# The experts' second layer as seven block products of half depth in place of four plain ones

## The chip, the cores and the metric

The kernel runs on one core of one Trainium2 chip. The metric is the device time of one launch in microseconds; lower is better. Engines are called PE (TensorE), DVE (VectorE), ACT (ScalarE), POOL (GpSimd) and SP (SyncE); the weight load of PE is PEld.

## What is computed

Two blocks follow each other on `x` of 32 sequences of 64 tokens of 1024 features. Cut to what matters here:

```python
x = x + ffn0(cond0(x))                       # mixing inside each sequence, then up/gate, silu, down
base_in = x @ W + lora(x)                    # "lin"
base  = einsum('bsi,oi->bso', base_in, W_org)
q     = einsum('bi,ki->bk', base_in.mean(axis=1), Wq)
coeffs = softmax(einsum('bk,ek->be', q, lora_keys) / sqrt(K))
h     = einsum('bsi,eir->bser', base_in, lora_down)        # 8 experts x rank 64 = 512 rows
delta = einsum('be,bser,ero->bso', coeffs, h, lora_up)     # the experts' second layer
x = x + base + delta
```

The second layer is one matrix product: 1024 outputs, depth 512 (expert and rank together), over the tokens, after `h` was scaled by the coefficients.

## The kernel before

The tokens are taken in two halves `h` of 1024, each in two tiles of 512. A half goes through a mixing step and six stages, `up0`, `up1`, `down`, `lin`, `exp` and `expup` (`STAGES`, line 55). `exp` is the joint stage: the base product and the experts' first layer together, on the same activations. `expup` is the experts' second layer.

**Block products.** A stage's product is cut in 2 x 2 blocks and done with seven block products instead of eight, from sums of weight blocks (T1 = w12 - w11, T2 = w22 - T1, T3 = w22 - w12, T4 = w21 - T2) and sums of activation blocks (S1 = a2 + a3, S2 = S1 - a0, S3 = a0 - a2, S4 = a1 - S2). Product 0 is w11 with a0, 1 is w21 with a1, 2 is T2 with S2, 3 is T1 with S1, 4 is w22 with S4, 5 is T3 with S3, 6 is T4 with a3. Products 0, 2, 3 and 4 (`IN_X`, line 44) add up in the same four PSUM banks without clearing them, 6 adds onto 5; after each one DVE adds what the banks hold into the output block `TO_BLOCK[i]`. So PE may go on to a bank only when DVE has read it (`wait_bank_free`, line 642; line 684 for this case). `expup` is the exception: it has four plain products of depth 512, no sums and no carried banks; `UP_TO_BLOCK` (line 48) names their output blocks. Below E0 to E3 are those four.

**Float32 by three passes.** Each operand is split in a rounded part and a rest. ACT makes the rounded part (`s_hi` line 813 from activations, `t_hi` line 832 from weights), DVE the rest (`s_lo`, `t_lo`, line 902), and PE multiplies hi by hi, hi by lo and lo by hi (lines 638 to 640). A product has four groups of output rows (six in `exp`), a group has four pieces of the depth, so twelve matmuls of 512 columns. `s_hi`/`s_lo` have two slots, `t_hi`/`t_lo` four slots of 128x1024.

**Order of the work.** PE, DVE and ACT each run one hand-written loop over all products (`for n in range(LAST + 1)`; DVE at line 1087). In the turn of product n DVE does, in this order: the second half's add of product n-1 (`dve_after`), the `s_lo` of n+1, the first weight rest of n+1, scalings of `dve_post`, the activation sums (`s_sum`, line 921), the weight sums (`t_sum`, line 945; in `exp` they come after the next step and the second weight rest), the add of the first half of n (line 1000, which waits for two groups of PE), further weight rests, and the add of the second half if `dve_own` gives it. Queues are in order: what waits holds back all behind it. `exp` scales the four expert blocks by the coefficients (line 1041), three of them in the turn of its last two products and one after its last.

**Loads and stores.** SP issues the weight loads in the order of its loop (line 544), each behind a wait that says its buffer is free (`load_w`, line 464; `load_x`, line 502, brings the next half's tokens). Around `expup` of the first half the order is: "lower" and "upper" (the two halves of `lora_up`, in buffers 3 and 1), four `x` pairs, "21" and "11" of the next `up0`; then "22", the last four `x` pairs, "12". POOL stores each finished output half block (line 613).

**Between the halves.** After `expup` of the first half PE does the mixing of the second (line 721): eight pairs of sequences, two banks each. Pairs 0 and 1 go to banks 0 to 3, pairs 2 and 3 to banks 4 to 7, and each waits for DVE's add of the last product that used its banks (line 731). In the same turn DVE makes the weight sums T1 and T2 of the next `up0` before its add of the last product's halves.

Of the kernel before, what the change touches and what calls it, by code (L numbers as in the profile page):

```python
# [47 lines left out]
UP_TO_BLOCK = (0, 2, 3, 1)  # L48
# [8 lines left out]
PRODUCTS = [(s, i) for s in range(NSTAGE) for i in range(4 if STAGES[s][1] == "expup" else 7)]  # L57
# [9 lines left out]
def groups_in(n):  # L67
    return 6 if kind_of(n) == "exp" else 4

# [15 lines left out]
S_ID, S_LAST = {}, []  # L85
T_ID, T_LAST = {}, []
for _n, (_s, _i) in enumerate(PRODUCTS):
    _up = kind_of(_n) == "expup"
    if _up and _i >= 2:
        S_ID[_n] = S_ID[_n - (1 if _i == 2 else 3)]  # L90
    else:
        S_ID[_n] = len(S_LAST)
        S_LAST.append(_n)
    S_LAST[S_ID[_n]] = _n
    for _j in range(groups_in(_n) // 2):
        if _up and _i % 2 == 1:
            T_ID[_n, _j] = T_ID[_n - 1, _j]
        else:
            T_ID[_n, _j] = len(T_LAST)
            T_LAST.append(None)  # L100
        T_LAST[T_ID[_n, _j]] = (_n, 2 * _j + 1)


def s_new(n):
    return S_LAST.index(S_LAST[S_ID[n]]) == S_ID[n] and not (kind_of(n) == "expup" and PRODUCTS[n][1] >= 2)


def t_halves(n, when):


    if kind_of(n) == "expup" and PRODUCTS[n][1] % 2 == 1:
        return []
    found = []
    for j in range(groups_in(n) // 2):
        before = T_LAST[T_ID[n, j] - 4] if T_ID[n, j] >= 4 else (-2, 0)
        if when == (0 if before[0] < n - 1 else before[1] // 2 + 1):
            found.append(j)
    return found
# [4 lines left out]
def t_sums_beside(n):  # L123
# [3 lines left out]
    if kind == "exp":  # L127
        found += {0: [(s, "T2", 0), (s, "T2", 1), (s, "T1", 2)], 1: [(s, "T2", 2)],
                  2: [(s, "T3", 0), (s, "T3", 1), (s, "T3", 2)],
                  4: [(s, "T4", 0), (s, "T4", 1), (s, "T4", 2)]}.get(i, [])  # L130
    elif kind != "expup":
        found += {3: [(s, "T3", 0), (s, "T3", 1)], 4: [(s, "T4", 0), (s, "T4", 1)]}.get(i, [])
    to = None
# [6 lines left out]
    elif to is not None and STAGES[to][1] != "expup":  # L140
# [42 lines left out]
def dve_after(n):  # L183
# [4 lines left out]
    return [] if kind == "expup" and i == 3 else dve_half(n, 1)  # L188
# [10 lines left out]
def dve_own(n):  # L199

    kind, i = kind_of(n), PRODUCTS[n][1]
    if kind == "exp" or kind == "expup" and i == 3:
# [49 lines left out]
SUMMED_STAGES = [s for s in range(NSTAGE) if STAGES[s][1] != "expup"]  # L252


def s_at(s, name):
    return 4 * SUMMED_STAGES.index(s) + S_ORDER[name]


def build(nc, x_pairs, x_t, idx, cond_t, b_upgate, b_down, lora_a, lora_b, keys_t, wq_t,
# [3 lines left out]
    with ExitStack() as ctx:  # L263
# [38 lines left out]
        a_raw = r[:, 8, :].rearrange("p (t n) -> p t n", t=TILES)  # L302
        t2_sb = we[:, 2:4, :].rearrange("p b n -> p (b n)")
# [37 lines left out]
        def act_blocks(s):  # L341

            h, kind = STAGES[s]
            if kind == "expup":
                return [r[:, 8, :], r[:, 9, :]]
# [21 lines left out]
        def bank_of(n, g):  # L367
            s, i = PRODUCTS[n]
            if STAGES[s][1] == "expup":
                return 4 * (i % 2) + g  # L370
# [20 lines left out]
        def t_source(n, j):  # L391
# [3 lines left out]
            if kind == "expup":  # L395
                return w_half((3, 3, 1, 1)[i], j)
# [27 lines left out]

        def wait_scaled(eng, s, t):

            h = STAGES[s][0]
            if t == 0:
                eng.wait_ge(summed, SUM_AT["scale", phase_of(h, "exp", 5), 1])
            else:  # L430
# [772 lines left out]
```

## Time and profile before

| what | value |
|---|---|
| median of 3 runs | 1003.94 us (1003.42 to 1004.28) |
| profiled execution, its own time | 1004.58 us |
| its span | 1002.9 us |
| PE busy | 992.4 us, 99% |
| DVE busy | 742.5 us, 74% |
| ACT busy | 391.4 us, 39% |
| POOL busy | 33.9 us, 3% |
| HBM read, written | 75.51 MB, 8.39 MB |

A busy share says what an engine had in hand, not that it was at its peak; matmul records overlap, since their ends are modelled. An idle engine costs something only where another one waits for it. In the rows, "idle before <-" names what ended an engine's idle time. A granted clock of 1.00 is TensorE at 2.4 GHz, 0.50 at 1.2 GHz.

### The profile page before, as it was taken

What the parts mean: (1) busy time and instruction counts of PE and PEld (TensorE: products, weight loads), DVE (VectorE), ACT (ScalarE), POOL (GpSimd) and SP (SyncE); (2) the same over time, 40 slices, a digit from 0 to 9 for tenths busy, and PEclk for the clock granted to TensorE, in tenths of its full rate; (3) what the DMA queues carried; (4) which work ended last, traced back from release to release, by engine and by line L of the source; (5) the groups of instructions that cost most, each with busy time, mean ns of one, the idle gap of its engine ahead of it and who ended that gap; (6) DMA issues with size and microseconds to landing.
All of it is one profiled execution on the core that took longest, in us unless ns stands there. A gap on an engine that the chain in (4) does not pass through costs nothing.

```text
span 1002.9 us, 12344 instructions
## 1 busy us (share of the span) xinstructions
PE 992.4 (99%) x4776; PEld 820.0 (82%) x4776; DVE 742.5 (74%) x574; ACT 391.4 (39%) x349; POOL 33.9 (3%) x55
## 2 busy tenths in 40 slices
PE   8999999999999999999999999999999999999997
PEld 6888888888887888888898888888888888888886
DVE  2877877998866889675446888789985859877641
ACT  6563563443344333331055544543433532423110
POOL 1600000000000000000100000000000000000011
PEclk9999999999999999999999999999999999999999
DMA  9022035025014001324311211521330230031012
GB/s 348 9 85 106 1 142 193 21 93 182 1 42 143 25 1 63 149 103 170 125 43 42 84 42 38 215 85 32 118 145 2 84 127 0 1 106 42 1 63 105
DMA packets 22985, 84.68 MB, mean 84 GB/s; under 512 B 2690, under 2 KB 6802, under 8 KB 17042
## 3 DMA queue, kind: packets, MB, share of 16 engines
q1 hardware_dynamic: 20450, 75.24, 20.8%
q0 software_dynamic: 2400, 8.41, 2.2%
q8 instruction: 39, 0.64, 0.3%
q10 hardware_dynamic: 80, 0.26, 0.1%
q14 instruction: 16, 0.13, 0.0%
HBM read 75.51 MB, written 8.39 MB: 84 GB/s over the span
## 4 chain that ended last, share of the span: by engine, by line
PE 98%; issue 1%; DMA 0%; DVEq 0%; DVE 0%; POOLq 0%; POOL 0%; SPq 0%
PE banks L638 31%; PE banks L639 31%; PE banks L640 31%; PE banks L734 3%; PE banks L699 2%; PE banks L717 1%; DMA cond_sb<-cond_t_in 0%; PE banks L746 0%; PE banks L760 0%; DVE r L1000 0%; DVEq L454 0%; POOLq L1137 0%; POOL out_t L621 0%; DVEq L457 0%; SPq L462 0%
## 5 line engine op out<-in xcount | busy, mean ns | idle before, releaser
L638 PE MATMUL banks<-s_hi,t_hi 128*128 128x512 f32 x1360 | 531.5, 391 | 0.0
L639 PE MATMUL banks<-s_lo,t_hi 128*128 128x512 f32 x1360 | 529.4, 389 | 0.0
L640 PE MATMUL banks<-s_hi,t_lo 128*128 128x512 f32 x1360 | 529.1, 389 | 0.0
L638 PEld LDWEIGHTS banks<-s_hi,t_hi 128*128 128x128 f32 x1360 | 255.2, 188 | 56.3 <-issue 3.6
L640 PEld LDWEIGHTS banks<-s_hi,t_lo 128*128 128x128 f32 x1360 | 255.3, 188 | 53.5
L639 PEld LDWEIGHTS banks<-s_lo,t_hi 128*128 128x128 f32 x1360 | 255.3, 188 | 52.3
L1000 DVE TENSOR_TENSOR r<-banks,r 128x1024 f32<-128x1024 f32 x92 | 111.5, 1219 | 100.3 <-PE banks L640 95.7
L902 DVE TENSOR_TENSOR t_lo<-w,t_hi 128x1024 fp32r<-128x1024 f32 x132 | 156.5, 1218 | 7.0 <-ACT t_hi L832 7.0
L813 ACT CAST s_hi<-st 128x2048 fp32r<-128x2048 f32 x40 | 76.5, 1913 | 197.7 <-PE banks L640 145.0
L832 ACT CAST t_hi<-w 128x1024 fp32r<-128x1024 f32 x132 | 133.3, 1048 | 50.4 <-PE banks L640 50.4
L813 ACT CAST s_hi<-r 128x2048 fp32r<-128x2048 f32 x34 | 65.0, 1913 | 203.3 <-PE banks L640 178.3
L902 DVE TENSOR_TENSOR s_lo<-st,s_hi 128x2048 fp32r<-128x2048 f32 x40 | 91.6, 2291 | 49.2 <-ACT s_hi L813 49.1
L902 DVE TENSOR_TENSOR s_lo<-r,s_hi 128x2048 fp32r<-128x2048 f32 x34 | 77.9, 2290 | 53.3 <-ACT s_hi L813 53.3
L984 DVE TENSOR_TENSOR w<-w 128x1024 f32<-128x1024 f32 x48 | 57.2, 1218 | 0.0
L832 ACT CAST t_hi<-we 128x1024 fp32r<-128x1024 f32 x30 | 30.9, 1052 | 60.0 <-PE banks L640 52.5
L844 ACT COPY r<-banks 128x1024 f32<-128x1024 f32 x40 | 40.4, 1010 | 21.6 <-PE banks L640 17.1
L1020 DVE TENSOR_TENSOR r<-banks,r 128x1024 f32<-128x1024 f32 x14 | 17.0, 1223 | 28.8 <-PE banks L640 28.8
L902 DVE TENSOR_TENSOR t_lo<-we,t_hi 128x1024 fp32r<-128x1024 f32 x30 | 35.9, 1219 | 0.0
L621 POOL DMA_DIRECT2D out_t<-r x16 | 11.7, 729 | 513.7 <-DVE r L1000 513.7
L862 ACT COPY r<-banks 128x1024 f32<-128x1024 f32 x16 | 15.9, 1013 | 29.0 <-PE banks L734 29.0
L1010 DVE SCALAR_TENSOR_TENSOR r<-banks,b_dn_sb,r 128x512 f32<-128x512 f32 x32 | 22.3, 743 | 4.6 <-PE banks L640 4.6
L936 DVE TENSOR_TENSOR st<-st,r 128x2048 f32<-128x2048 f32 x10 | 23.0, 2295 | 1.0
(63 smaller groups left out, 358.2 us busy)
## 6 DMA issues: line engine op xcount, KB each, us to landing
w<-w_up_in SPq DMA_DIRECT2D x16, 1024.0 KB, 4.8
w<-w_base_in SPq DMA_DIRECT2D x10, 1024.0 KB, 4.8
w<-w_down_in SPq DMA_DIRECT2D x8, 1024.0 KB, 5.2
r<-x_t_in SPq DMA_DIRECT2D x8, 1024.0 KB, 6.2
w<-w_lin_in SPq DMA_DIRECT2D x8, 1024.0 KB, 5.4
out_t<-r POOLq DMA_DIRECT2D x16, 512.0 KB, 3.2
we<-w_expin_in SPq DMA_DIRECT2D x10, 512.0 KB, 4.6
st<-x_pairs_in SPq DMA_DIRECT2D x8, 512.0 KB, 7.2
```

What stands on the lines that cost most here:

```text
L638: pe.matmul(out, w_hi, x_hi, start=start, stop=False, skip_group_check=True)
L639: pe.matmul(out, w_hi, x_lo, start=False, stop=False, skip_group_check=True)
L640: return pe.matmul(out, w_lo, x_hi, start=False, stop=stop, skip_group_check=True)
L734: last = pe.matmul(out[:, k, :], x_pair(c)[:, k * P:(k + 1) * P], mix[:, c, :], start=True, stop=True)
L813: act.copy(s_hi[:, S_ID[n] % 2, :], s_source(n)).then_inc(s_hi_done, 1)
L832: act.copy(t_hi[:, T_ID[n, j] % 4, :], t_source(n, j)).then_inc(t_hi_done, 1)
L844: act.copy(half_block(n, at), half_banks(n, at)).then_inc(snapped, 1)
L902: return dve.tensor_tensor(out, value, hi.bitcast(F32), ALU.subtract)
L936: dve.tensor_tensor(upper, lower, a[0], ALU.subtract).then_inc(s_made, 1)
L984: dve.tensor_tensor(out, left, right, ALU.subtract).then_inc(t_made, 1)
L1000: dve.tensor_tensor(half_block(n, at), half_banks(n, at), half_block(n, at), ALU.add).then_inc(summed, 1)
L1010: dve.scalar_tensor_tensor(out=group_block(n, at), in0=banks[:, bank_of(n, at), :], scalar=b_dn_sb[:, m:m + 1], in1=group_block(n, at), op ...
```

## The change

`expup` becomes seven block products as in the other stages, each of half the depth (256, two pieces instead of four), E0 to E6 below. It has its own activation sums S1 to S4 and weight sums T1 to T4, of 128x1024 each, kept in the tile `we`. T1, T2 and T3 are made by DVE in the turn of the last product of `exp` (exp6), T4 in the turn of E1. `lora_up` is laid out anew in DRAM so that "lower" holds w11 and w21 and "upper" w12 and w22. An activation split fills half a slot; a weight split one slot of which a group uses 256 columns. The waits that free buffers name other products: "22" of the next `up0` now waits for the weight rest of E6 (before: of E0), "12" for that of E5 (before: of E2), the last four `x` pairs for the `s_lo` of E5 and E6 (before: of E0 and E1). The order of SP's loads stays.

```diff
-PRODUCTS = [(s, i) for s in range(NSTAGE) for i in range(4 if STAGES[s][1] == "expup" else 7)]
+PRODUCTS = [(s, i) for s in range(NSTAGE) for i in range(7)]
...
+def chunks_in(n):
+    return 2 if kind_of(n) == "expup" else 4
...
     elif kind != "expup":
         found += {3: [(s, "T3", 0), (s, "T3", 1)], 4: [(s, "T4", 0), (s, "T4", 1)]}.get(i, [])
+    elif i == 1:
+        found += [(s, "T4", 0)]
...
+    elif to is not None and STAGES[to][1] == "expup":
+        found += [(to, "T1", 0), (to, "T2", 0), (to, "T3", 0)]
...
     kind, i = kind_of(n), PRODUCTS[n][1]
-    if kind == "exp" or kind == "expup" and i == 3:
+    if kind == "exp" or kind == "expup" and i == 6:
         return [dve_half(n, 0), dve_half(n, 1)]
     return [dve_half(n, 0), []]
...
+        up_w11, up_w21, up_w12, up_w22 = (w[:, b, j * 8 * P:(j + 1) * 8 * P] for b in (3, 1) for j in range(2))
+        up_t1, up_t2 = we[:, 2, :], we[:, 3, :]
...
             if kind == "expup":
-                return w_half((3, 3, 1, 1)[i], j)
+                return (up_w11, up_w21, up_t2, up_t1, up_w22, up_w12, up_w21)[i]
...
+        def s_sums(s):
+
+            return (we[:, 0, :], we[:, 1, :]) if STAGES[s][1] == "expup" else (st[:, 0, :], st[:, 1, :])
...
                     else:
-                        sp.wait_ge(t_ready, t_at(FIRST[s - 1] + (0 if block == "22" else 2), 1))
+                        sp.wait_ge(t_ready, t_at(FIRST[s - 1] + (6 if block == "22" else 5), 0))
...
                 if h > 0:
-                    last = ("exp", 5) if c < 2 else ("exp", 4) if c < 4 else ("expup", 0) if c < 6 else ("expup", 1)
-                    sp.wait_ge(s_ready, S_ID[phase_of(h - 1, *last)] + 1)
+                    last = ("exp", 5) if c < 2 else ("exp", 4) if c < 4 else ("expup", 5 if c < 6 else 6)
+                    sp.wait_ge(s_ready, phase_of(h - 1, *last) + 1)
...
-                for u in range(4):
+                for u in (1, 4, 5, 6):
                     store(h, u, 0)
                     store(h, u, 1)
...
-                if kind == "expup":
-                    if i == 0:
-                        wait_taken(pe, phase_of(h, "exp", 5 if g < 2 else 6), 4 + g % 2)
-                    elif i == 1:
-                        wait_taken(pe, phase_of(h, "exp", 6), g)
-                    else:
-                        wait_taken(pe, n - 2, g)
+                if kind == "expup" and i == 0:
+                    wait_taken(pe, phase_of(h, "exp", 5 if g < 2 else 6), 4 + g % 2)
...
                         for g in (bank % 4, bank % 4 + 1):
-                            wait_taken(pe, phase_of(h - 1, "expup", 2 if bank < 4 else 3), g)
+                            wait_taken(pe, phase_of(h - 1, "expup", 4 if bank < 4 else 6), g)
...
-                    fresh = g >= 4 or kind == "expup" or i in (0, 1, 5)
+                    fresh = g >= 4 or i in (0, 1, 5)
                     begun = lora and g >= 2
-                    for p in range(4):
-                        last = product(n, g, p, fresh and p == 0 and not begun, p == 3)
+                    for p in range(chunks_in(n)):
+                        last = product(n, g, p, fresh and p == 0 and not begun, p == chunks_in(n) - 1)
...
-                if kind != "expup":
-                    for name in {0: ("S1", "S2"), 2: ("S4",), 3: ("S3",)}.get(i, ()):
-                        s_sum(s, name)
+                for name in {0: ("S1", "S2"), 2: ("S4",), 3: ("S3",)}.get(i, ()):
+                    s_sum(s, name)
```

DVE in the first half, from the scaling after the last group of exp6 on, before. `r<-r,coef` is the scaling, `r<-banks,r` the adds of an output half (the first two rows of them are E0's two halves, then come E1's two and E2's two), `t_lo<-w` a weight rest.

```order
L1041 TENSOR_TENSOR r<-r,coef 128x1024
L902 TENSOR_TENSOR s_lo<-r,s_hi 128x2048
L1000 TENSOR_TENSOR r<-banks,r 128x1024 x2
L902 TENSOR_TENSOR t_lo<-w,t_hi 128x1024 x2
L1000 TENSOR_TENSOR r<-banks,r 128x1024 x4
```

The same place after (L1010 is the add, L928, L932 and L936 the activation sums S1, S2 and S4, L994 the weight sum T4):

```order
L897 TENSOR_TENSOR s_lo<-r,s_hi 128x1024
L928 TENSOR_TENSOR we<-r 128x1024
L932 TENSOR_TENSOR we<-we,r 128x1024
L1010 TENSOR_TENSOR r<-banks,r 128x1024 x2
L897 TENSOR_TENSOR s_lo<-we,s_hi 128x1024
L897 TENSOR_TENSOR t_lo<-we,t_hi 128x1024
L994 TENSOR_TENSOR w<-w,we 128x1024
L1010 TENSOR_TENSOR r<-banks,r 128x1024 x2
L897 TENSOR_TENSOR s_lo<-we,s_hi 128x1024
L897 TENSOR_TENSOR t_lo<-w,t_hi 128x1024
L936 TENSOR_TENSOR we<-r,we 128x1024
L1010 TENSOR_TENSOR r<-banks,r 128x1024 x2
```

Between the scaling and the add of E2's first half there stood seven instructions, one of them a split of double width, in the time of two products of 48 matmuls; now thirteen stand there, in the time of two products of 24, and the last row's first add is that of E2's first half.

DVE at the joint between the halves, before, with the waits (the four L984 rows are T1 and T2 of the next `up0`; `w_loaded1` is the load of "12", `w_loaded3` that of "22"):

```order
L1000 TENSOR_TENSOR r<-banks,r 128x1024 [waits summed,group_done] x4
L902 TENSOR_TENSOR t_lo<-w,t_hi 128x1024 [waits t_hi_done] x2
L984 TENSOR_TENSOR w<-w 128x1024 [waits t_ready,w_loaded1]
L984 TENSOR_TENSOR we<-w 128x1024 [waits t_ready,t_made,w_loaded3]
L984 TENSOR_TENSOR w<-w 128x1024 [waits t_ready,w_loaded1]
L984 TENSOR_TENSOR we<-w 128x1024 [waits t_ready,t_made,w_loaded3]
L1000 TENSOR_TENSOR r<-banks,r 128x1024 [waits summed,group_done] x2
L902 TENSOR_TENSOR s_lo<-r,s_hi 128x2048 [waits s_hi_done] x2
```

And after:

```order
L897 TENSOR_TENSOR s_lo<-r,s_hi 128x1024 [waits s_hi_done]
L1010 TENSOR_TENSOR r<-banks,r 128x1024 [waits summed,group_done] x2
L897 TENSOR_TENSOR t_lo<-w,t_hi 128x1024 [waits t_hi_done] x2
L994 TENSOR_TENSOR w<-w 128x1024 [waits t_ready,w_loaded1]
L994 TENSOR_TENSOR we<-w 128x1024 [waits t_ready,t_made,w_loaded3]
L994 TENSOR_TENSOR w<-w 128x1024 [waits t_ready,w_loaded1]
L994 TENSOR_TENSOR we<-w 128x1024 [waits t_ready,t_made,w_loaded3]
L1010 TENSOR_TENSOR r<-banks,r 128x1024 [waits summed,group_done] x2
L897 TENSOR_TENSOR s_lo<-r,s_hi 128x2048 [waits s_hi_done] x2
```

The order of the last eight rows is as it was; what moved is the `s_lo` of the last product, whose end now frees the last `x` pairs and so the load of "12" behind them, to just ahead of them.

## Rows read from the trace of the kernel before

**Rows 1.** Page, part 1: busy time, share of the span and instructions of each engine.

```profile
PE 992.4 (99%) x4776; PEld 820.0 (82%) x4776; DVE 742.5 (74%) x574; ACT 391.4 (39%) x349; POOL 33.9 (3%) x55
```

**Rows 2.** Page, part 4: the chain that ended last, by engine.

```profile
PE 98%; issue 1%; DMA 0%; DVEq 0%; DVE 0%; POOLq 0%; POOL 0%; SPq 0%
```

**Rows 3.** Timeline of PE inside a stage: start us, us, engine, line, operation.

```profile
379.70 0.39 PE L639 MATMUL banks<-s_lo,t_hi 128*128 128x512 f32 x1
...
401.46 0.39 PE L639 MATMUL banks<-s_lo,t_hi 128*128 128x512 f32 x1
```

**Rows 4.** Stretches, us: busy (x) of PE, PEld, DVE, ACT, POOL, clock, DMA, GB/s.

```profile
346.40:460.60 114.20, 114.20 (x516) 94.46 (x515) 87.60 (x71) 34.34 (x30) 0.00 (x0) 1.00 0.24 88
460.62:504.14 43.52, 43.52 (x194) 36.05 (x193) 22.39 (x19) 5.92 (x5) 5.12 (x7) 1.00 0.34 121
```

**Rows 5.** Timeline of DVE, first half, end of exp to the mixing.

```profile
444.30 2.35 DVE L1020 TENSOR_TENSOR r<-banks,r 128x1024 f32<-128x1024 f32 x2 [0.81 <-PE banks L640]
446.57 2.28 DVE L902 TENSOR_TENSOR s_lo<-r,s_hi 128x2048 fp32r<-128x2048 f32 x1
...
455.18 1.22 DVE L1000 TENSOR_TENSOR r<-banks,r 128x1024 f32<-128x1024 f32 x1 [1.79 <-PE banks L640]
460.62 1.23 DVE L1020 TENSOR_TENSOR r<-banks,r 128x1024 f32<-128x1024 f32 x1 [4.21 <-PE banks L640]
461.95 1.23 DVE L1041 TENSOR_TENSOR r<-r,coef 128x1024 f32<-128x1024 f32 x1
...
496.67 1.22 DVE L984 TENSOR_TENSOR w<-w 128x1024 f32<-128x1024 f32 x1
497.97 1.23 DVE L984 TENSOR_TENSOR we<-w 128x1024 f32<-128x1024 f32 x1
...
504.14 1.23 DVE L1000 TENSOR_TENSOR r<-banks,r 128x1024 f32<-128x1024 f32 x1 [1.35 <-PE banks L640]
```

**Rows 6.** Timeline of ACT: the split that waited for that scaling.

```profile
463.26 1.91 ACT L813 CAST s_hi<-r 128x2048 fp32r<-128x2048 f32 x1 [12.47 <-DVE r L1041]
```

**Rows 7.** Timeline of PE: the mixing between the halves, and the next stage's first matmul.

```profile
503.94 7.30 PE L734 MATMUL banks<-mix,st 128*128 128x128 f32 x64
...
518.15 0.48 PE L638 MATMUL banks<-s_hi,t_hi 128*128 128x512 f32 x1
```

**Rows 8.** DMA, 0:24: GB/s in 40 slices.

```profile
GB/s 0 0 0 27 266 341 239 191 273 321 239 328 375 410 416 416 430 464 423 423 416 396 416 437 410 416 403 410 421 411 385 387 390 423 423 437 437 423 396 396
```

**Rows 9.** Timeline of SP: the issue of "12" of the second half's up0.

```profile
475.01 0.34 SPq L487 DMA_DIRECT2D w<-w_up_in  x1
```

**Rows 10.** Page, part 6: DMA issues, KB each, us from issue to landing.

```profile
w<-w_up_in SPq DMA_DIRECT2D x16, 1024.0 KB, 4.8
...
out_t<-r POOLq DMA_DIRECT2D x16, 512.0 KB, 3.2
```

**Rows 11.** Timeline of PE: the last matmul.

```profile
996.86 0.39 PE L640 MATMUL banks<-s_hi,t_lo 128*128 128x512 f32 x1
```

**Rows 12.** Stretches: first mixing, and behind the last matmul (columns as Rows 4).

```profile
8.00:10.00 2.00, 1.49 (x7) 1.52 (x8) 0.39 (x2) 1.97 (x3) 0.46 (x2) 1.00 1.03 422
10.00:12.00 2.00, 2.00 (x11) 2.00 (x11) 0.00 (x0) 1.77 (x3) 0.46 (x2) 1.00 1.03 432
12.00:13.00 1.00, 1.00 (x7) 1.00 (x6) 0.00 (x0) 0.70 (x1) 0.23 (x1) 1.00 1.00 418
14.00:16.00 2.00, 2.00 (x20) 2.00 (x20) 0.00 (x0) 1.39 (x2) 1.65 (x7) 1.00 1.02 414
999.60:999.80 0.20, 0.00 (x0) 0.00 (x0) 0.00 (x0) 0.00 (x0) 0.20 (x1) 0.60 0.00 0
```

**Rows 13.** Timeline of DVE, second half, the end.

```profile
953.77 1.23 DVE L1020 TENSOR_TENSOR r<-banks,r 128x1024 f32<-128x1024 f32 x1 [4.22 <-PE banks L640]
...
997.29 1.22 DVE L1000 TENSOR_TENSOR r<-banks,r 128x1024 f32<-128x1024 f32 x1 [4.21 <-PE banks L640]
```

**Rows 14.** Timeline of POOL: the last store's issue.

```profile
999.15 0.72 POOL L621 DMA_DIRECT2D out_t<-r  x1 [5.04 <-DVE r L1000]
```

More of the change, by code:

```diff
@@ L80, in groups_of, with t_half_of @@
     return range(2 * j, 2 * j + 2)
-S_ID, S_LAST = {}, []
-T_ID, T_LAST = {}, []
+S_PLACE, S_AFTER = {}, {}
+T_ID, T_LAST, T_WHEN = {}, [], {}
+_turn, _users = 0, {}
 for _n, (_s, _i) in enumerate(PRODUCTS):
-    _up = kind_of(_n) == "expup"
-    if _up and _i >= 2:
-        S_ID[_n] = S_ID[_n - (1 if _i == 2 else 3)]
-    else:
[L92 to L97, printed above, removed]
-        else:
[L99 to L105, printed above, removed]
-def t_halves(n, when):
[L111 to L118, printed above, removed]
+    if kind_of(_n) == "expup":
+        S_PLACE[_n] = ((_turn + _i // 2) % 2, _i % 2)
+        _halves = [S_PLACE[_n]]
+    else:
+        S_PLACE[_n] = (_turn, 0)
+        _halves = [(_turn, 0), (_turn, 1)]
+        _turn = 1 - _turn
+    S_AFTER[_n] = max(_users.get(_half, -1) for _half in _halves)
+    _users.update((_half, _n) for _half in _halves)
+    for _j in range(1 if kind_of(_n) == "expup" else groups_in(_n) // 2):
+        _id = T_ID[_n, _j] = len(T_LAST)
+        T_LAST.append((_n, 3 if kind_of(_n) == "expup" else 2 * _j + 1))
+        _last = T_LAST[_id - 4] if _id >= 4 else (-2, 0)
+        _beside = _n - 2 if kind_of(_n) == "expup" and _i > 0 else _n - 1
+        if kind_of(_n) == "expup" and _i == 2:
+            _beside = _n - 3
+        T_WHEN[_n, _j] = (_beside, 0 if _last[0] < _beside else _last[1] // 2 + 1)
+def t_halves(n, when):
+    return [half for half in T_ID if T_WHEN[half] == (n, when)]
+def t_half_of(n, g):
+    return 0 if kind_of(n) == "expup" else g // 2
 def t_sums_beside(n):
@@ L344, in act_blocks @@
             if kind == "expup":
-                return [r[:, 8, :], r[:, 9, :]]
+                return [e_block(b) for b in range(4)]
             base = first_block(h, kind in ("up0", "up1", "lin"))
@@ L909, in s_split, with t_split @@
             def s_split(n):
-                if not s_new(n):
-                    return
-                dve.wait_ge(s_hi_done, S_ID[n] + 1)
-                lo(s_lo[:, S_ID[n] % 2, :], s_source(n), s_hi[:, S_ID[n] % 2, :]).then_inc(s_ready, 1)
-            def t_split(n, when):
-                for j in t_halves(n, when):
+                dve.wait_ge(s_hi_done, n + 1)
+                slot, cols = s_place(n)
+                lo(s_lo[:, slot, cols], s_source(n), s_hi[:, slot, cols]).then_inc(s_ready, 1)
+            def t_split(beside, when):
+                for n, j in t_halves(beside, when):
                     slot = T_ID[n, j] % 4
@@ L923, in s_sum @@
                 h, kind = STAGES[s]
[L924 removed]
+                lower, upper = s_sums(s)
                 if name == "S1":
@@ L954, in t_sum @@
                     loaded = {b: (w_loaded[b_at], LOAD_AT[s, b]) for b, b_at in W_BUFFER.items() if (s, b) in LOAD_AT}
-                if name == "T1":
+                if name == "T1" and kind == "expup":
+                    e = phase_of(h, "exp", 0)
+                    dve.wait_ge(*loaded["11"])
+                    dve.wait_ge(*loaded["12"])
+                    dve.wait_ge(t_made, TMADE_AT[s - 1, "T4", 2])
+                    dve.wait_ge(t_ready, t_at(e + 2, 2))
+                    out, left, right = up_t1, w12, w11
+                elif name == "T1":
                     dve.wait_ge(*loaded["12"])
@@ L961, in t_sum @@
                     dve.wait_ge(t_made, TMADE_AT[s, "T1", j])
-                    if kind == "exp":
+                    if kind == "expup":
+                        dve.wait_ge(t_ready, t_at(phase_of(h, "exp", 4), 2))
+                        out, left, right = up_t2, w22, up_t1
+                    elif kind == "exp":
                         dve.wait_ge(t_ready, t_at(n + 1, j))
```

130 lines of the change are left out of this document (60 added, 70 removed).

## The prediction

> **What bounds the kernel now.** I read the page's busy shares first, then the chain of waits, then the timelines around the last stage. PE is busy 99% of the span and the chain that ended last is 98% PE [rows 1, 2]: the reader is to see that PE never waits for anybody, so a matmul taken away is worth its full spacing as long as nobody else becomes late. That spacing is not the 391 ns of the records, which overlap: 96 matmuls from 379.70 to 401.46 are 0.2267 us each [rows 3]. The stage to be changed lasts from 460.62, where DVE sees the last group of exp6, to 504.14, where it sees the last of the old E3: 43.52 us = 192 x 0.2267 [rows 4, 5]. DVE is at half load there (22.4 of 43.5 us), but at 87.6 of 114.2 us in `exp` [rows 4]. So there is room in the sum; whether it is in the right place must be followed instruction by instruction.
>
> **What is removed.** 7 x 4 groups x 2 pieces x 3 = 168 matmuls stand for 4 x 4 x 4 x 3 = 192. 24 x 0.2267 = 5.44 us less per half, 10.88 in all. A product now lasts 24 x 0.2267 = 5.44 us, a group 1.36.
>
> **What is added, on DVE.** Per half 14 adds for 8, seven weight rests for four, seven half-width activation rests for two of full width, eight sums for none. In a row of queued instructions of 128x1024 one starts every 1.135 us (444.30 to 446.57 for two), a 2048-wide one measures 2.28 and the half of it is taken as 1.135 too; one that needs its forerunner's result starts 1.30 to 1.33 after it [rows 5]. Together 14 + 7 + 7 + 8 = 36 instructions, some 41 us, for 38.1 us of PE. Six of them (the weight rests of E0, E1 and E2, and T1 to T3) lie in the turn of exp6, with the `s_lo` of E0. DVE's idle gaps there are 1.79 us before 455.18 and 4.21 before 460.62 [rows 5], 6.0 in all; three sums and one more rest are 4.5 us and the halved `s_lo` gives 1.1 back. So exp6 hides them: cost nothing, if 2.6 us of cover vanished it would start to cost. ACT's splits (14 of some 1.05 us) fall in its gaps: it waited 12.5 us there before one of them [rows 6].
>
> **The queue of DVE in the stage.** From 460.62: the add to the expert block, the scaling at 461.95, then without a gap `s_lo` E1, S1, S2, E0's two adds, `s_lo` E2, `t_lo` E3, T4, E1's two adds, `s_lo` E3, `t_lo` E4, S4, E2's first add. That last one is 14 instructions behind the scaling: 461.95 + 14 x 1.135 + 0.16 (S2 on S1) = 478.0, done 479.2. PE runs E0 from 460.62 (its `s_lo` is ready by 447.7), E1 from 466.06 (ready 464.3), E2 from 471.50 (ready 470.2). E3 could go on at 476.94, but it adds onto the banks of E2, which DVE takes only by 479.2. After a wait I count 0.3: a matmul that follows on has its record 0.20 before the group is seen done (503.94 and 504.14 [rows 5, 7]), and a semaphore takes about 0.08 (DVE done 463.18, ACT at 463.26 [rows 5, 6]). E3 starts at 479.5: **2.6 us of stall**. E4 waits for E3's first add in the same way (`s_lo` E4, `t_lo` E5 and S3 stand before it; done 484.9, PE free 485.0 and up at 485.2): **0.24**. From there DVE has fewer extras: E5 begins at 490.7 (its `s_lo` 487.4), E6 at 496.1 (`s_lo` 493.0, banks 494.6) and ends at 501.5. Bounds of the first stall: 2.3, if PE follows at once, to 3.8, if each of the 14 steps takes the full 1.22 us of an instruction [rows 5]. Per half -5.44 + 2.84 = -2.6.
>
> **The second half** has nothing behind it but the last store. From 953.77 to 997.29 it is the same 43.52 us [rows 13], so the end moves by -2.6. The last store goes out 2.72 us behind the one before it, which takes 3.2 to land [rows 10, 14]: 0 to 0.5 us more, taken at 0.
>
> **The joint after the first half.** Here a load decides. "12" of the next `up0` was issued at 475.01 [rows 9] and T1 used it at 496.67. Now SP waits at "22" for the weight rest of E6 (488.5), sends two `x` pairs, then waits at the last two for the `s_lo` of E6 (493.0), and only then sends "12". From 489.5 to its landing 4.2 MB of loads go (1.05 for "22", 2.1 for the four pairs, 1.05 for "12"), beside the stores of E4 and E5's first half, 1.6 MB. The engines together moved about 420 GB/s when fully loaded [rows 8]. 5.8 MB take 13.7 us: 503. Without any share for the stores it is 499.5 plus a landing, about 500.3; with all of the next store too 504.4. I take 502.9, near the end at which the stores move beside the loads, as the nearest rows have no burst in which a store stood back.
> The Trainium skill, DMA: Bandwidth & Descriptors (Queues, rings and completion order) says that each DMA engine serves the queues that have work in turn. By that rule the loads get the larger part but not all, between the two ends above.
> DVE reaches T1 at 499.5 and waits until 503.0. T1, T2, T1, T2 take 1.30 + 1.15 + 1.31 + 1.14 = 4.9 (496.67 to 501.57 in the trace, whose first step is 1.30 [rows 5]), then E6's first add ends at 509.1. PE does two pairs of the mixing from 501.5, 1.78 us each (14.21 / 8 [rows 7]), and at 505.1 needs banks 4 and 5, which that add frees: on at 509.4. **Stall 4.3 us.** It is 0.8 if the load is early, 1.8 at 500.3 and 5.8 at 504.4. Behind it the mixing paces all: the next `s_lo` has 1.5 us of slack in the order that stays.
>
> **The clock.** A pause of PE has a second price. The last matmul ends at 997.25 and the granted clock falls from 1.00 (2.4 GHz) to 0.50 (1.2 GHz) inside 999.6 to 999.8, 2.4 us later [rows 11, 12]. The mixing's pause, from the record's end at about 505.2 to 509.2, is 4.0 us, longer; E3's, from 477.1 to 479.3, is 2.2 us, just shorter. What the low clock costs shows at the start, after PE's first pause: 25 records of the mixing between 8.5 and 13, against 20 in 2 us later [rows 12] (the column prints 1.00 where no event is on record; the spacing shows the low level). 4.5 us for 2.5 us of work: **2.0 us**, with 1.5 to 2.8 as bounds.
> The Trainium skill, TensorE: Matmul & The Clock Gate (HAM oscillation), says that a wait for a transfer between groups of matmuls can put the array back to 1.2 GHz, and that it is paid at every such wait. The rows agree for the end of the kernel; by that rule the mixing pays, as I count it.
>
> **Sum.** First half -5.44 + 2.84 + 4.3 + 2.0 = +3.7; second half -2.6; together +1.1. On the profiled execution, 1004.58 with a span of 1002.9, that is 1005.7 with a span of 1004.0. It stood 0.64 above the median of 1003.94, so the median becomes **1005.0**. A measurement of this kernel can tell about 0.2%, 2.0 us, from no change: the forecast lies within it.
>
> **Rivals.**
> A, the joint's pause does not lower the clock: all but the 2.0, 1003.0. For it: a single row shows the fall, and PE has work on both sides of the pause. Chance 0.22; forecast 0.38.
> B, the load of "12" is early enough (stores yield to loads, or DVE is later at T1): the joint stalls 0.8 to 1.8 us and the clock stays. Two halves of -2.6 plus 0.8 to 1.8 are -4.4 to -3.4: 999.5 to 1000.5. Against it: the bytes. Chance 0.14.
> C, on the slow side: E3's pause of 2.2 us lowers the clock too, in one half or both. Place: between E2 and E3; price 2.0 each, since a product at 1.2 GHz takes nearly twice its time until the clock is back; it decides from a pause a few tenths longer than I work out, and the fall came 2.4 after the last matmul. 1007.0 for one, 1009.0 for both. Chance 0.21.
> The Trainium skill, same page (A second HAM failure mode), says that short idles between groups, from cycling through banks, are enough to make the clock swing. That is this rival as a rule; no row here shows it.
> D, DVE's chain is no bound (the adds run ahead, the sums hide): all 10.88 come in, 993.1. It needs the 14 instructions to pass in less than 14.9 us; the rows speak against it. Chance 0.05.
>
> **Numbers.** The range takes in A, B, the forecast and C with one fall, 1000.0 to 1008.0; D, C with both and an edge of B stay out, under 0.2. Faster by over 2.0: D, B and an early-load edge of A, 0.22. Slower by over 2.0: C and the late-load edge of the forecast (each us of landing is one of time), 0.33. Within: 0.45.
>
> **What would show it.** In the trace after: PE idle some 2.5 us ahead of E3 behind DVE's add in both halves; DVE waiting 3 to 4 us at the T1 sum for the DMA of "12"; PE idle some 4 us between the second and third pair of the mixing, and the clock at 0.50 after it; DVE all but full from 460 to 480. I am wrong if DVE does not wait at T1 (then B), if the clock is 0.50 inside the stage (C), or if `exp` gets longer.

## The result: 1009.65 us, slower by 0.68%

| what | before | after |
|---|---|---|
| median | 1003.68 us (1003.0 to 1004.28, 4 runs) | 1009.65 us (1009.33 to 1012.11, 4 runs) |
| ratio to before, 95% interval | | 1.0068 (1.0056 to 1.008) |
| span of the profiled execution | 1002.9 us | 1007.8 us |
| matmuls on PE | 4776 | 4728 |

The range 1000.0 to 1008.0 did not hold it, and where a change within the noise was forecast (+1.1 us), the kernel is slower by 6.0. The page of the changed kernel, part 1 and the chain that ended last (part 4), against [rows 1, 2]: PE is 7 us less busy in a span that is 5 us longer, and the chain can be followed back only to 509.9 (49% of the span), where DVE makes the last weight sum ahead of E6's adds and PE waits for these.

```profile
PE 985.6 (98%) x4728; PEld 813.7 (81%) x4728; DVE 787.8 (78%) x618; ACT 403.7 (40%) x365; POOL 35.8 (4%) x55
...
PE 46%; DVE 2%; issue 1%; POOLq 0%; POOL 0%; DVEq 0%
```

The list of waits (who waited for whom: us, times, longest) has three rows that before did not have:

```profile
PE banks L735 <- DVE r L1010: 8.2, 1, 8.2
DVE w L994 <- DMA w<-w_up_in: 7.3, 1, 7.3
...
PE banks L644 <- DVE r L1010: 5.0, 2, 2.5
```

The timeline of DVE, first half (against [rows 5]); L1030 is the add after exp6's last group, L994 the weight sums of the next `up0`, L1010 the adds:

```profile
459.59 1.22 DVE L1030 TENSOR_TENSOR r<-banks,r 128x1024 f32<-128x1024 f32 x1 [2.45 <-PE banks L646]
...
476.99 2.35 DVE L1010 TENSOR_TENSOR r<-banks,r 128x1024 f32<-128x1024 f32 x2
...
496.33 2.35 DVE L897 TENSOR_TENSOR t_lo<-w,t_hi 128x1024 fp32r<-128x1024 f32 x2
505.96 1.22 DVE L994 TENSOR_TENSOR w<-w 128x1024 f32<-128x1024 f32 x1 [7.28 <-DMA w<-w_up_in]
...
510.87 2.35 DVE L1010 TENSOR_TENSOR r<-banks,r 128x1024 f32<-128x1024 f32 x2
```

And of PE (against [rows 7]): the first matmul of E3, the mixing in its pieces, the first of `up0`:

```profile
478.36 0.47 PE L644 MATMUL banks<-s_hi,t_hi 128*128 128x512 f32 x1 [2.49 <-DVE r L1010]
```

```profile
500.44 3.73 PE L735 MATMUL banks<-mix,st 128*128 128x128 f32 x32
512.35 6.36 PE L735 MATMUL banks<-mix,st 128*128 128x128 f32 x32 [8.18 <-DVE r L1010]
518.54 7.31 PE L735 MATMUL banks<-mix,r 128*128 128x128 f32 x64
525.60 0.48 PE L644 MATMUL banks<-s_hi,t_hi 128*128 128x512 f32 x1
```

The reader is to see where the time went. From exp6's last group to the mixing it is 500.44 - 459.59 = 40.85 us, before 503.94 - 460.62 = 43.32: 2.47 gained. The mixing, to the first matmul of `up0`, is 25.16 us for 14.21: 10.95 lost. The second half's last stage (DVE's add at 961.21, the last at 1002.26, 41.05 us) gains 2.47 on [rows 13]. Together +6.0; the medians differ by 5.97. The two profiled executions differ only by 4.96 (1009.54 for 1004.58), because exp6's last group came 1.03 earlier in this one. What lies between the two stages (from the first matmul of `up0` to DVE's add at 961.21, before at 953.77) took 435.6 us in both.

Stretches of 2 us in the mixing (busy of PE, PEld, DVE, ACT, POOL, then the clock): the pause, and the clock at 0.50, 1.2 GHz.

```profile
506.00:508.00 2.00, 0.00 (x0) 0.00 (x0) 1.91 (x2) 0.00 (x0) 0.00 (x0) 0.86 0.00 0
508.00:510.00 2.00, 0.00 (x0) 0.00 (x0) 1.91 (x3) 0.00 (x0) 0.00 (x0) 0.50 0.00 0
...
516.00:518.00 2.00, 2.00 (x13) 2.00 (x13) 0.00 (x0) 1.01 (x1) 0.00 (x0) 0.58 0.30 113
```

The mixing's 10.95 are therefore 8.3 of pause (pair 2 could have begun at 500.44 + 3.57 = 504.0, it began at 512.35) and 2.6 of low clock (pairs 2 and 3 took 518.54 - 512.35 = 6.19 us instead of 3.57).

What held DVE is "12". T3 and T4 of `expup` are not in `we`, other than said above: they overwrite w12 and w21 in buffers 1 and 3, the buffers of the next "12" and "22". That is why "22", which goes first, must wait for the weight rest of E6. The issue of "12" on SP, and the DMA traffic of the stretch 485:509 (GB/s in 40 slices of 0.6 us, totals, loads in q1, stores in q0):

```profile
493.17 0.48 SPq L491 DMA_DIRECT2D w<-w_up_in  x1
```

```profile
GB/s 0 0 27 0 0 14 177 232 423 437 382 225 307 253 266 328 437 416 430 417 410 410 416 423 437 430 423 464 382 416 457 410 437 225 0 0 0 0 0 0
DMA packets 1441, 6.31 MB, mean 263 GB/s; under 512 B 160, under 2 KB 160, under 8 KB 1184
...
q1 hardware_dynamic: 864, 4.19, 47.3%
q0 software_dynamic: 576, 2.10, 21.4%
```

12.8 us from issue to landing, where [rows 10] had 4.8 as the median of 16 loads.

### The profile page after: what moved, and what is told of

Same layout as the page of the kernel before. It is cut to its first block and busy times, and to the rows that moved or that the text cites. A ratio compares the mean times of both kernels' runs of the same rounds, so it can differ in the third digit from the quotient of the medians.

```text
span 1007.8 us, 12376 instructions
## 1 busy us (share of the span) xinstructions
PE 985.6 (98%) x4728; PEld 813.7 (81%) x4728; DVE 787.8 (78%) x618; ACT 403.7 (40%) x365; POOL 35.8 (4%) x55
## 5 line engine op out<-in xcount | busy, mean ns | idle before, releaser
L644 PE MATMUL banks<-s_hi,t_hi 128*128 128x512 f32 x1344 | 525.5, 391 | 5.0 <-DVE r L1010 5.0
L645 PE MATMUL banks<-s_lo,t_hi 128*128 128x512 f32 x1344 | 523.3, 389 | 0.0
L646 PE MATMUL banks<-s_hi,t_lo 128*128 128x512 f32 x1344 | 523.0, 389 | 0.0
L1010 DVE TENSOR_TENSOR r<-banks,r 128x1024 f32<-128x1024 f32 x104 | 125.3, 1218 | 61.6 <-PE banks L646 57.0
L811 ACT CAST s_hi<-r 128x2048 fp32r<-128x2048 f32 (+1 forms) x36 | 63.7, 1769 | 178.4 <-PE banks L646 178.2
L897 DVE TENSOR_TENSOR s_lo<-r,s_hi 128x2048 fp32r<-128x2048 f32 (+1 forms) x36 | 76.0, 2111 | 48.8 <-ACT s_hi L811 48.8
L994 DVE TENSOR_TENSOR w<-w 128x1024 f32<-128x1024 f32 x50 | 59.6, 1218 | 7.3 <-DMA w<-w_up_in 7.3
L830 ACT CAST t_hi<-we 128x1024 fp32r<-128x1024 f32 x34 | 35.1, 1053 | 68.7 <-PE banks L646 61.2
L897 DVE TENSOR_TENSOR t_lo<-we,t_hi 128x1024 fp32r<-128x1024 f32 x34 | 40.8, 1218 | 0.0
L1030 DVE TENSOR_TENSOR r<-banks,r 128x1024 f32<-128x1024 f32 x14 | 17.0, 1223 | 25.3 <-PE banks L646 25.3
L735 PE MATMUL banks<-mix,st 128*128 128x128 f32 x128 | 20.0, 333 | 9.4 <-DVE r L1010 8.2
L735 PEld LDWEIGHTS banks<-mix,st 128*128 128x128 f32 x128 | 19.7, 247 | 11.3 <-issue 8.3
```

What stands on the lines that cost most here:

```text
L644: pe.matmul(out, w_hi, x_hi, start=start, stop=False, skip_group_check=True)
L645: pe.matmul(out, w_hi, x_lo, start=False, stop=False, skip_group_check=True)
L646: return pe.matmul(out, w_lo, x_hi, start=False, stop=stop, skip_group_check=True)
L735: last = pe.matmul(out[:, k, :], x_pair(c)[:, k * P:(k + 1) * P], mix[:, c, :], start=True, stop=True)
L811: act.copy(s_hi[:, slot, cols], s_source(n)).then_inc(s_hi_done, 1)
L830: act.copy(t_hi[:, T_ID[n, j] % 4, :], t_source(n, j)).then_inc(t_hi_done, 1)
```

## The experiments

All are changes of the changed kernel. The theory: two places where PE waits for DVE's queue, one inside the stage (in front of E3), one in the mixing; the second is long because a load is late; and such a wait can lower the clock. The rivals stand in each expectation. In this section a time without more is the median; the kernel before stood at 1003.21 to 1003.37 beside them.

### The load of "12" first

```diff
-                    load_w(s + 1, "22")
+                    load_w(s + 1, "12")
+                    load_w(s + 1, "22")
                     for c in range(4, PAIRS):
                         load_x(h + 1, c)
-                    load_w(s + 1, "12")
```

> SP issues "12" of the next up0 ahead of "22" and the last four x pairs; nothing else changes. Theory (the late landing of "12" holds DVE's weight sums, these hold E6's adds, PE pauses 8.3 us in the mixing and the clock falls): "12" is issued at about 482 and lands before DVE reaches T1, DVE does not wait for a DMA, the mixing pauses under 1.5 us behind the four sums, the clock stays at 1.00; the two stalls of 2.5 us ahead of E3 stay. Time 1009.65 - 7.4 - 2.6 = 999.7, between 998.5 and 1001. Rival (the mixing waits for its x pairs or for the adds themselves, whatever "12" does): pause and time stay, 1009 to 1010, or the pause moves to the x pairs, which now go out behind 2 MB.

1001.33 us (999.7 to 1002.5, 10 runs), 0.9981 of before (0.9971 to 0.999). DVE's first weight sum came without a wait, and PE's pause between pairs 1 and 2 was 0.8:

```profile
498.64 1.22 DVE L994 TENSOR_TENSOR w<-w 128x1024 f32<-128x1024 f32 x1
```

```profile
505.02 3.81 PE L735 MATMUL banks<-mix,st 128*128 128x128 f32 x32 [0.81 <-DVE r L1010]
```

The profiled execution took 999.7, as expected, the others 0.8 to 2.8 more, at mean clocks of 0.995 to 0.998 for 0.999. The runs on E3's wait below suggest that these are falls of the clock there; for this kernel it is not shown. The rival falls: the load decides.

### The weight sums last

```diff
-                if kind != "exp":
+                sums_last = kind == "expup" and i == 6
+                if kind != "exp" and not sums_last:
                     for what in t_sums_beside(n):
                         t_sum(*what)
                 if not own_first:
                     take(dve_own(n)[0])
...
                 take(dve_own(n)[1])
+                if sums_last:
+                    for what in t_sums_beside(n):
+                        t_sum(*what)
```

> DVE makes T1 and T2 of the next up0 after E6's two adds instead of before; the loads stay as they are, so "12" still lands at about 506. Theory: DVE still waits for "12" some 5 us, but with nothing behind it that PE needs soon; no pause in the mixing, clock 1.00; 1009.65 - 8.3 - 2.6 = 998.7, between 998 and 1000. Rival (the load, and not its place in DVE's queue, is what costs; or the transfers slow the mixing): the pause stays, above 1004.

1000.79 us (998.39 to 1001.72, 10 runs), 0.9971 (0.9961 to 0.9982). The load landed even later (47.7 us behind exp6's last group, for 46.4), DVE waited for it 5.4 us, and PE went through the mixing without a pause:

```profile
507.21 1.22 DVE L994 TENSOR_TENSOR w<-w 128x1024 f32<-128x1024 f32 x1 [5.44 <-DMA w<-w_up_in]
```

```profile
500.35 7.31 PE L735 MATMUL banks<-mix,st 128*128 128x128 f32 x64
```

So it is not the late load in itself: it costs only through what DVE has queued behind it. Three of the ten executions were at 998.4 to 998.6, seven at 1000.7 to 1001.7, and nothing in between.

### PE kept busy in the mixing's pause

```diff
+                            if c == 2 and g == 0:
+                                pe.wait_ge(mixed_copied, h * PAIRS + 2)
+                                for _ in range(30):
+                                    pe.matmul(banks[:, 0, 0:P], x_pair(0)[:, 0:P], mix[:, 0, :], start=True, stop=True)
                             wait_taken(pe, phase_of(h - 1, "expup", 4 if bank < 4 else 6), g)
```

> In the second mixing PE runs 30 extra matmuls of 128 columns on a bank that was already copied, after pair 1's copy and before the wait for pair 2's banks (results unused). All waits stay. Theory (the pause lowers the clock and that costs 2.6 us of the 11 lost in the mixing): clock 1.00 through the mixing, pairs 2 and 3 take 3.6 us instead of 6.2, time 1009.65 - 2.6 = 1007.0, with 1006.5 to 1007.7. Rival (the clock falls for another reason, or the slow pairs are slow for the transfers beside them): 1009 to 1010, clock at 0.50 after 507 as before.

1008.67 us (1008.57 to 1010.85, 4 runs): outside what was expected, 1.7 above its middle. The mechanism was there: the extra matmuls (L735 here) fill the pause, the clock stays, and pairs 2 and 3 take 517.64 - 513.99 = 3.65 us instead of 6.19.

```profile
506.93 6.94 PE L735 MATMUL banks<-mix,st 128*128 128x128 f32 x60 [1.19 <-ACT r L864]
513.99 3.81 PE L739 MATMUL banks<-mix,st 128*128 128x128 f32 x32
517.64 7.31 PE L739 MATMUL banks<-mix,r 128*128 128x128 f32 x64
```

The difference lies earlier, as far as the profile shows it. In this execution the clock fell at E3, in the stretches around its start:

```profile
478.00:480.00 2.00, 1.48 (x6) 1.23 (x7) 2.00 (x3) 1.32 (x2) 0.00 (x0) 0.88 0.00 0
480.00:482.00 2.00, 2.00 (x6) 1.60 (x5) 2.00 (x3) 0.00 (x0) 0.00 (x0) 0.50 0.00 0
```

From exp6's last group to the `s_lo` of E6, DVE needed 492.46 - 459.75 = 32.71 us instead of 490.89 - 459.59 = 31.30: 1.4 us for it. In the second half of the same execution the same wait of 2.49 us left the clock at 1.00. In the profile of the changed kernel both halves kept it.

### The stores held back

```diff
                 for u in (1, 4, 5, 6):
+                    if h == 0 and u == 4:
+                        pool.wait_ge(w_loaded[1], LOAD_AT[stage_of(1, "up0"), "12"])
                     store(h, u, 0)
```

> POOL holds the stores of E4, E5 and E6 of the first half until "12" has landed; SP's order and waits stay. Theory (6.3 MB of loads and stores fill the DMA engines; the stores' 2.1 MB are a third of the 12.8 us that "12" takes to land): 4.2 MB at some 410 GB/s from 489, "12" lands at 499.5 to 500.5 instead of 505.9, DVE waits 1.5 us at T1, the mixing pauses 2.5 to 3 us, the clock stays or falls for a shorter time: 1009.65 - 5.5 = 1004.1 with a fall, 1001.5 without. Rival ("12" is late because it is issued late and its x neighbours' form is slow, stores do not matter): landing at 504 to 506, time above 1008.

1005.74 us (1003.79 to 1008.67, 10 runs), between the theory's 1004.1 and the rival's 1008. The profiled execution is the slowest of the ten. In it "12" took 9.0 us from issue to landing instead of 12.8. Less than expected: the stores are 3.8 us of it, and the expectation had put the start of the loads where the other profile had it, while here everything ran 2.6 later (1.2 from the start of the program, 1.4 in the stage). Nor did the loads run at 410 GB/s without the stores. The DMA traffic of 485:509 again, in slices of 0.6 us; from 491.0 to 503.0 it is the 4.2 MB of loads alone, at 348 GB/s on average:

```profile
GB/s 0 0 0 0 0 0 0 0 0 0 137 109 341 437 437 341 389 410 444 382 164 205 369 396 430 423 437 444 423 246 27 27 0 0 0 307 396 260 396 369
```

DVE's wait and PE's pause in the mixing:

```profile
PE banks L737 <- DVE r L1012: 4.2, 1, 4.2
...
DVE w L996 <- DMA w<-w_up_in: 3.3, 1, 3.3
```

The 1.4 are E3's wait of 2.5 us again, which here lowered the clock in both halves; two stretches of the first and two of the second half:

```profile
480.00:482.00 2.00, 2.00 (x8) 1.57 (x7) 2.00 (x3) 0.37 (x1) 0.00 (x0) 0.68 0.00 0
482.00:484.00 2.00, 2.00 (x6) 1.51 (x6) 1.95 (x2) 0.00 (x0) 0.00 (x0) 0.50 0.00 0
...
978.00:980.00 2.00, 2.00 (x8) 1.62 (x7) 2.00 (x3) 0.50 (x1) 0.00 (x0) 0.76 0.00 0
980.00:982.00 2.00, 2.00 (x6) 1.53 (x5) 2.00 (x2) 0.00 (x0) 0.00 (x0) 0.50 0.00 0
```

Six matmul records in 2 us, where a stretch at full clock has ten. It is the rival C of the prediction, by its own rows. The second half's stage took 1001.39 - 958.93 = 42.46 us for 41.05: 1.4 for it there too.

### The adds of E2 and E3 first, T4 later

```diff
-    elif i == 1:
+    elif i == 3:
         found += [(s, "T4", 0)]
...
-                own_first = kind == "down" and i in (3, 6)
+                own_first = kind == "down" and i in (3, 6) or kind == "expup" and i in (2, 3)
```

> DVE's order inside the new stage: E2's and E3's first add ahead of the sums S4 and S3, and T4 one turn pair later (in E3's turn). The joint's order and the loads stay. Theory (E3 waits for DVE's queue, 14 instructions of 1.135 us behind the scaling): E2's first add stands two places earlier, E3's wait falls from 2.5 to about 0.3 us, the clock cannot fall there, the joint keeps its 8 us and its fall: 1009.65 - 2 x 2.3 = 1005.0, between 1004.3 and 1005.8. Rival (the later instructions only move the wait to E4 or E5): under 1 us gained in all, above 1008.5.

1007.61 us (1007.41 to 1007.78, 4 runs): a miss, between the two expectations. The waits inside the stage did fall, from 2.5 to 0.4 at most, but those at the joint grew by one microsecond each:

```profile
PE banks L735 <- DVE r L1010: 9.2, 1, 9.2
...
DVE w L994 <- DMA w<-w_up_in: 8.3, 1, 8.3
...
PE banks L644 <- DVE r L1010: 1.2, 4, 0.4
```

Two things were missed. In the stage E3 waits 0.22 us, but the second half of E4 waits 0.42 for E3's second add, which now stands behind S3 and T4: the stage is shorter by 1.43 us in each half (from exp6's last group to the last add 1000.28 - 960.66 = 39.62 us, for 41.05), not by 2.3. And in the first half even that did not all arrive. The mixing began 1.43 us earlier after exp6's last group, "12" was used only 0.42 earlier (505.71 - 459.76 for 505.96 - 459.59), and the first matmul of `up0` came 0.71 earlier. 1.43 + 0.71 = 2.14, by the medians 2.04. The expectation had added up gains along two paths: the joint is set by the loads, and these start at E6's weight rest, which DVE makes at the same time in either order.

### T4 later, on the kernel with the weight sums last

```diff
-    elif i == 1:
+    elif i == 3:
         found += [(s, "T4", 0)]
```

> On the kernel with the weight sums last (998.4 to 998.6 or 1000.7 to 1001.7, median 1000.8): T4 made in E3's turn instead of E1's, nothing else. Theory (PE is paced by DVE's queue up to E3's first add, where the same 21 instructions stand before and after): E3's wait is 1.1 us shorter and E4's 1.1 us longer, the sum stays 2.6; but no wait is long enough to lower the clock, so all executions lie at 998.3 to 999.3. Rival 1 (each instruction taken from ahead of E2's add is a net gain): 996.5. Rival 2 (the clock falls by the sum of the idle time in a stretch, not by one wait): median stays 1000.8.

997.78 us (997.58 to 999.09, 4 runs), for 1000.79. PE's first matmuls of E3 and of E4:

```profile
476.19 0.47 PE L644 MATMUL banks<-s_hi,t_hi 128*128 128x512 f32 x1 [1.36 <-DVE r L1010]
...
482.99 0.47 PE L644 MATMUL banks<-s_hi,t_hi 128*128 128x512 f32 x1 [1.08 <-DVE r L1010]
```

One wait of 2.49 became two of 1.36 and 1.08: one place earlier in DVE's queue is 1.13 us, and the sum is 2.44, nearly what it was. PE waits as long as before in all, and yet the median is 3.0 lower. The clock is at 1.00 around both waits in the profile, and all four executions have a mean clock of 0.999. None lay above 999.1.

### PE kept busy ahead of E3

Also on the kernel with the weight sums last:

```diff
+                    if kind == "expup" and i == 3 and g == 0:
+                        for j in range(2):
+                            wait_taken(pe, n - 2, 2 * j)
+                        for _ in range(10):
+                            slot, cols = s_place(n)
+                            pe.matmul(banks[:, 4, :], t_hi[:, T_ID[n, 0] % 4, 0:P], s_hi[:, slot, cols.start:cols.start + TN],
+                                      start=True, stop=True, skip_group_check=True)
                     wait_bank_free(n, g)
```

> The kernel with the weight sums last, which ran at 998.4 to 998.6 in three executions and at 1000.7 to 1001.7 in seven, with ten extra matmuls (results unused) in PE's wait ahead of E3, 2.27 us; all waits stay. Theory (the wait of 2.5 us lowers the clock in most executions, and that is the difference between the two kinds): all executions at 998.3 to 999.3, median 998.6. Rival (the two kinds have another cause, such as the mixing's transfers): the spread stays and the median is 1000.5 to 1001.

999.21 us (997.99 to 999.34, 5 runs). The kind at 1001 is gone although the wait of 2.5 us is still there and ten matmuls more are done. The median lies at the upper edge of what was expected. With the run before it this leaves the clock at E3 as the cause of the two kinds; no profile of an execution at 1001 exists, so it rests on the times, the mean clocks and these two runs. The seven executions mean 1001.1 us at a mean clock of 0.996 to 0.997, the three 998.5 at 0.999: 2.6 us, which fits one fall in each half.

### "12" ahead of the last two pairs only

```diff
-                    for c in range(4, PAIRS):
-                        load_x(h + 1, c)
-                    load_w(s + 1, "12")
+                    load_x(h + 1, 4)
+                    load_x(h + 1, 5)
+                    load_w(s + 1, "12")
+                    load_x(h + 1, 6)
+                    load_x(h + 1, 7)
```

> SP sends "12" behind "22" and the x pairs 4 and 5, but ahead of pairs 6 and 7, whose wait for E6's rest comes 3.5 us later. Bytes, stores and DVE stay. Theory (its place behind two pairs that wait costs most of the 12.8 us, the stores the rest): issued at 489.5, 3.1 MB of loads and about 1 MB of stores from 488.9 at 370 GB/s, landing at 498.5 to 500.5; DVE waits 0 to 2 us, the mixing 1 to 2.5 us, clock 1.00 there; time 1000 to 1002.5, as with "12" first. Rival (the bytes decide, wherever it stands): landing after 503, time above 1004.

1004.77 us (1003.72 to 1007.52, 10 runs). The landing came just past the late end of what was worked out: issued at 488.69, used at 500.65, DVE's wait 2.2. The time is a miss, 2.3 above the range and in the rival's: the mixing's pause was 3.1 us, longer than worked out, and the clock fell behind it, so that pairs 2 and 3 took 5.28 us (512.32 - 507.04) for 3.57.

```profile
500.65 1.23 DVE L996 TENSOR_TENSOR w<-w 128x1024 f32<-128x1024 f32 x1 [2.20 <-DMA w<-w_up_in]
```

```profile
506.00:508.00 2.00, 0.96 (x4) 0.99 (x5) 1.92 (x2) 0.00 (x0) 0.72 (x1) 0.76 0.00 0
508.00:510.00 2.00, 2.00 (x12) 2.00 (x11) 0.00 (x0) 0.00 (x0) 0.72 (x1) 0.50 0.76 277
```

The clock fell a second time in this execution, behind E3's wait in the second half, and not in the first half. A stretch of each; the waits were 2.50 and 2.49 us:

```profile
480.00:482.00 2.00, 2.00 (x10) 1.66 (x9) 2.00 (x3) 0.00 (x0) 0.00 (x0) 1.00 0.00 0
...
976.00:978.00 2.00, 2.00 (x6) 1.52 (x6) 2.00 (x2) 0.00 (x0) 0.00 (x0) 0.50 0.03 8
```

The second half's stage took 42.46 us for 41.05, the same 1.4 as in the two runs above.

Counted from exp6's last group (459.34 here) the load was used 5.1 us earlier than in the changed kernel. It was issued 4.2 us earlier, since it no longer stands behind the two pairs that wait for E6, and the transfer itself still took 12.0 us, for the 2.1 MB ahead of it and the stores beside it.

### All three together, and the order of DVE alone

The sums last, the adds of E2 and E3 first with T4 later, and the `s_lo` of E1 made in DVE's idle time ahead of exp6's last group; the first of the two also with "12" first.

```diff
-                if n < LAST and kind_of(n + 1) != "up0" or i < 6 and kind == "up0":
+                if (n < LAST and kind_of(n + 1) != "up0" or i < 6 and kind == "up0") and not (kind == "expup" and i == 0):
                     s_split(n + 1)
...
+                if kind == "exp" and i == 6:
+                    s_split(n + 2)
```

> "12" first, the weight sums behind E6's adds, E2's and E3's adds first with T4 later, and the activation rest of E1 in DVE's idle time before exp6's last group. Theory: no wait of PE above 0.4 us in the stage or the mixing, clock 1.00 to the end; both halves give their 5.44 us: 1003.4 - 10.9 = 992.5, with up to 1.2 us for the x pairs' landing: 992.3 to 994. Rival (another bound takes over, ACT's splits or the x pairs of the mixing): 995 to 998.

993.58 us (992.85 to 995.23, 4 runs), 0.9905 of before (0.9888 to 0.9921), inside what was expected.

> As the one with all three but with SP's loads in the order of the changed kernel: DVE's order alone. Theory (a late "12" costs nothing once nothing that PE needs is queued behind it): DVE waits some 3 us for "12" inside the mixing and PE does not notice; 992.5 to 994, equal to the other within 1 us. Rival (the load's landing still paces something): over 995.

993.68 us (992.63 to 994.53, 4 runs), 0.9901 (0.9884 to 0.9917), also inside. Its DVE waited 6.6 us for the load, and the mixing ran without a pause. But PE did notice in the profiled execution, behind the mixing: the first matmul of `up0` waited 0.8 us for its activation rest, which stands behind the four sums in DVE's queue, and from the start of the mixing to that matmul it was 15.29 us for 14.21 in the other kernel. The medians, 0.1 apart in runs that spread over some 2 us, can't tell this.

```profile
DVE w L994 <- DMA w<-w_up_in: 6.6, 1, 6.6
...
PE banks L644 <- DVE s_lo L897: 0.8, 1, 0.8
```

Both beat the kernel before by 9.5 to 9.6 us of the 10.88 that the removed matmuls are worth; of all kernels here they are the fastest. Against the changed kernel the second one differs in DVE's order alone: no instruction was saved.

## Why the prediction was wrong, point by point

**The matmuls' worth** held: 48 fewer, 5.44 us per half; the last two kernels bring 9.5 to 9.6 of the 10.88 us.

**exp hides the added sums**: right. DVE still waited 2.45 us for exp6's last group, against 2.6 of cover worked out.

**DVE's queue in the stage**: right to a tenth. E2's first add, 14 instructions of 1.135 us behind the scaling, stood at 476.99 = 460.92 + 16.07, worked out as 16.05; E3's wait was 2.49 and the loss with the refill about 2.7 for 2.6; E4's 0.1 to 0.2 for 0.24. The net gain per half was 2.47 for 2.6. The run with T4 later shows the price per place, 1.13 us.

**The landing of "12"** is the step that failed, by its size. The prediction said 502.9 with 504.4 as the late end. On its time scale (exp6's last group at 460.62, in the profile after at 459.59) the load was used at 507.0. The order of the transfers and their start were right; the bytes and the rate were not:

- It counted three stores beside the loads; all four of E4 and E5 went through, 6.3 MB, not 5.8. At its 420 GB/s that is 1.2 us.
- It took 420 GB/s for the whole of it, which [rows 8] show only from their eleventh busy slice on; the ten ahead of it have 27 to 375. Here too the first ten slices from 488.6 on have 177 to 437, 303 on average, and those after them 382 to 464 until the traffic ends. The slow 6 us cost 1.7 us against 420. In all, 6.3 MB took some 17 us, about 370 GB/s.
- It gave the last bytes no time to be seen by DVE (some 0.7 us here), and took 502.9 where its own sum gives 503.3.

Why the rate is low in the first part stays open. Loads and stores run together there, but so they do later at 382 to 464, and the loads without stores had only 348 on average. The other two runs price single causes: 3.8 us for all stores, 5.1 for sending "12" ahead of two pairs. These are no parts of the 4.1 us: the place behind the pairs and three of the stores were in the prediction's sum.

The miss of 4.1 us passed on to PE nearly one for one: a pause of 8.3 for 4.3. With 0.6 more of low clock and 0.3 less gained in the two stages it makes the 4.9 between the forecast change of +1.1 and the measured +6.0. The median missed 1005.0 by 4.65, since the kernel before measured 0.26 lower this time.

**The clock in the mixing**: right in kind, 2.6 for 2.0, inside its bounds of 1.5 to 2.8. Where the pause was shorter the cost was smaller: 1.7 us in the profiles with the stores held and with "12" ahead of two pairs, whose pauses were 4.2 and 3.1 us. The run with PE kept busy shows the price: 6.19 against 3.65 us for the same two pairs.

**Rival C** was the one to weigh more. In the four executions measured with the change it can have decided only in one, 1012.11 against 1009.3 to 1009.8; but in the kernels that share the stage unchanged, E3's wait lowered the clock in seven of ten executions with the sums last, by their times and mean clocks, and in four of the twelve halves of the six profiles that have the wait of 2.49. The argument that 2.2 us of pause is shorter than the 2.4 seen behind the last matmul took one event for a threshold. Its price was worked out as 2.0 each and measured as 1.3 (half of the 2.6 between the two kinds of executions) to 1.4 (the profile with PE kept busy).

**What would show it** all came: DVE waits at T1 (7.28 for 3 to 4), PE pauses in the mixing (8.18 for 4), the clock at 0.50.

## What to carry to other kernels

A plan that halves the size of the steps halves the time in which the other engine's queue must turn around, even if that engine's total load still fits: count the instructions between a result and the one that frees it, in the order of the queue. A wait that is moved to a later event moves every load queued behind it too, and an in-order engine that waits for such a load should have nothing behind it that the bounding engine needs soon. Moving such work back only moves the wait: with DVE's order alone the first matmul of `up0` met it, for 0.8 us. What was lost here was had back, and more, by order alone.

## What the runs showed of the hardware

A single wait of PE of 2.49 us lowered the granted clock from 1.00 to 0.50 in some places and not in others of the same program, even within one execution (with PE kept busy in the mixing's pause only the first half fell, with "12" ahead of two pairs only the second), for a loss of 1.3 to 1.4 us each. By the mean clocks of the stretches, the fall came 0.9 to 1.3 us after PE had begun again (estimates from the four falls behind E3's wait: with the stores held, the mean of 0.68 in 480:482 is 1.3 us at 0.50, so the clock fell at 480.7, and PE had begun at 479.56). Some 2.44 us of waiting split in 1.36 and 1.08 lowered it in none of four executions. Matmuls whose results nobody uses, put into the wait, kept the clock up (999.21 for 1000.79 us, and 3.65 for 6.19 us in the mixing). And a load of 1 MB that lands in 4.8 us in the median of the kernel before took 12.8 behind the other loads of this place and beside four stores, and 9.0 without the stores.
